# A graph attention pass on one core: the expanded target values are summed on TensorE, not on VectorE

## The reference, cut to what matters

```python
h = (x @ W).reshape(n, HEADS, HID)
src = jnp.concatenate([edge_index[0], loops])
dst = jnp.concatenate([edge_index[1], loops])
a_src = jnp.einsum('nhf,hf->nh', h, att_src)
a_dst = jnp.einsum('nhf,hf->nh', h, att_dst)
e = jax.nn.leaky_relu(a_src[src] + a_dst[dst], NEG_SLOPE)
m = jax.ops.segment_max(e, dst, num_segments=n)
ex = jnp.exp(e - m[dst])
denom = jax.ops.segment_sum(ex, dst, num_segments=n)
alpha = ex / denom[dst]
msg = h[src] * alpha[:, :, None]
agg = jax.ops.segment_sum(msg, dst, num_segments=n)
```

## Time and profile before

| | |
|---|---|
| time, 3 runs | 8511.83 us median, 8507.89 to 8514.34 |
| profiled execution, its own time | 8512.61 us |
| its span | 8510.8 us |
| busy | PE 5215.0 us, DVE 5632.1 us, ACT 3045.4 us, POOL 6107.9 us |
| granted clock of TensorE, mean | 0.755 |
| first attention pass | gathers of POOL from 2426.6 to 3591.1 us, last totals from 3654.0 us |

### The profile page before, as it was taken

The page is one execution under the profiler, slowest core; times in us unless marked ns, Lnnn a source line. Parts: engine busy times, 40 slices in busy tenths (PEclk is TensorE's granted clock), DMA queues, the critical chain, the costliest instruction groups (busy, mean ns, idle before and its releaser), DMA issues. The chain is left out here.

```text
span 8510.8 us, 132427 instructions
## 1 busy us (share of the span) xinstructions
PE 5215.0 (61%) x35514; PEld 4581.5 (54%) x35514; DVE 5632.1 (66%) x13509; ACT 3045.4 (36%) x7001; POOL 6107.9 (72%) x5620
## 2 busy tenths in 40 slices
PE   0991014444367777664444425565579898989896
PEld 0340013333345555453333325565579898989896
DVE  9661025555578888664444465555579898989898
ACT  2000002000048888632222222222156666666564
POOL 4777777777647777637777727777768787878785
PEclk7995555555578888786666657667689999999998
DMA  1671025565645555723333424444567676767674
GB/s 43 268 307 61 2 61 130 130 145 131 112 118 138 140 140 137 119 68 79 82 82 79 75 56 130 130 130 130 118 182 223 188 222 189 222 188 223 190 221 138
DMA packets 963123, 1176.14 MB, mean 138 GB/s; under 512 B 286490, under 2 KB 845422, under 8 KB 949342
## 3 DMA queue, kind: packets, MB, share of 16 engines
q1 hardware_dynamic: 806782, 864.50, 33.2%
q0 software_dynamic: 155616, 303.19, 16.8%
HBM read 897.16 MB, written 269.96 MB: 137 GB/s over the span
## 5 line engine op out<-in xcount | busy, mean ns | idle before, releaser
L2584 PE MATMUL ps<-u,wide_r 128*128 x9280 | 1141.8, 277 | 128.7 <-issue 88.6
L2584 PEld LDWEIGHTS ps<-u,wide_r 128*128 128x128 f32 x9280 | 1093.4, 194 | 130.7 <-issue 130.7
L2159 POOL DMA_INDIRECT z_r<-x_tab,src_row x880 | 851.9, 968 | 417.6 <-issue 267.8
L2596 PE MATMUL ps<-msg_r,hots_r 128*128 128x128 f32 x9280 | 1135.6, 275 | 21.6 <-POOL msg_r L2417 21.6
L2417 POOL TENSOR_TENSOR msg_r<-zo_r,share_r 128x1024 f32<-128x1024 f32 x580 | 1123.4, 1937 | 11.9 <-DVE share_r L2469 9.5
L1362 POOL DMA_INDIRECT ring_e<-t_tab,src_p x928 | 882.9, 951 | 298.8 <-issue 280.7
L2596 PEld LDWEIGHTS ps<-msg_r,hots_r 128*128 128x128 f32 x9280 | 1082.5, 192 | 26.4 <-POOL msg_r L2417 25.5
L296 POOL DMA_INDIRECT rec_tab<-pay,row_i x831 | 806.3, 970 | 372.6 <-issue 272.2
L541 POOL DMA_INDIRECT ring<-y_tab,y_row x880 | 842.8, 958 | 276.1 <-issue 263.4
L2425 POOL TENSOR_TENSOR prod_r<-prod_r 128x512 f32<-128x512 f32 x580 | 735.4, 1268 | 415.3 <-DVE prod_r L2447 414.0
L1779 POOL DMA_INDIRECT ring_e<-t_tab,src_row x880 | 830.7, 944 | 271.8 <-issue 267.8
(11 more groups left out here) (321 smaller groups left out, 9329.9 us busy)
## 6 DMA issues: line engine op xcount, KB each, us to landing
zo_r<-zo_tab SPq DMA_DIRECT2D x2320, 192.0 KB, 2.8
y_tab<-wide SPq DMA_DIRECT2D x100, 1024.0 KB, 3.9
zo_tab<-z_r SPq DMA_DIRECT2D x110, 512.0 KB
hot_bytes_e<-hb_tab SPq DMA_DIRECT2D x464, 64.0 KB
dl_b<-dl_tab SPq DMA_DIRECT2D x220, 128.0 KB, 3.7
zo_tab<-hot_bytes SPq DMA_DIRECT2D x220, 128.0 KB
hb_tab<-hot_bytes SPq DMA_DIRECT2D x220, 128.0 KB
hot_bytes_e<-hb_tab SPq DMA_DIRECT2D x55, 512.0 KB
```

The costliest lines, as they stand in the source:

```text
L2159: nc.gpsimd.indirect_dma_start(out=z[:, g % ZR, c, :], out_offset=None, in_=x3_tab, in_offset=bass.IndirectOffsetOnAxis(ap=src_row[:, g * ...
L2584: last = nc.tensor.matmul(ps[:, 2 * (g % 2) + c // 4, c % 4 * D:(c % 4 + 1) * D], wide[:, g % WR, c, :], u[:, bass.ds(tiles[g % NO % 4 * O ...
L2596: last = nc.tensor.matmul(ps[:, 4 + g % 2, c // 2 * D:(c // 2 + 1) * D], hots[:, g % WR, c, :], msg[:, g % WR, c, :], start=c % 2 == 0, st ...
```

## The change

The three parts of a value are no longer written beside one another and added by DVE. `expand` makes three matmuls of 8 columns a place, one for each part k, into the same 8 columns of PSUM: the first starts the sum (`start=k == 0`), the others add to it. The result, 16 places x 8 values, stands in columns 256 to 383 of the bank; the turned parts in columns 0 to 255 and the exponentials from column 384 stay where they were. The reduction on DVE, its semaphore `s_sent` and its SBUF tile `sent` are gone, and L1465 and L1471 read the sums from PSUM. The order in which the functions are called is the same on every engine.

```diff
-                SW = 3 * 2 * HEADS
-
-                def expanded(b):
-                    return ps[:, 6 + b % 2, 0:BC * SW]
+                def sent_of(b):
+                    return ps[:, 6 + b % 2, 256:256 + BC * 2 * HEADS].rearrange("p (c w) -> p c w", w=2 * HEADS)
...
-                            v.tensor_reduce(sent[:].rearrange("p c w -> p (c w)"),
-                                            expanded(b).rearrange("p (c k w) -> p c w k", c=BC, k=3),
-                                            AX.X, ALU.add).then_inc(s_sent, 1)
-                            dve.wait_ge(s_sent, b + 1)
-                            v.tensor_tensor(sc, sent[:, :, 0:HEADS], ring[:, b % ZR, :, hf:W], ALU.add)\
+                            v.tensor_tensor(sc, sent_of(b)[:, :, 0:HEADS], ring[:, b % ZR, :, hf:W], ALU.add)\
...
-                            v.tensor_tensor(sc, sc, sent[:, :, HEADS:2 * HEADS], ALU.subtract).then_inc(s_sc, 1)
+                            v.tensor_tensor(sc, sc, sent_of(b)[:, :, HEADS:2 * HEADS], ALU.subtract).then_inc(s_sc, 1)
...
                             for c in range(BC):
-                                last = nc.tensor.matmul(
-                                    expanded(b)[:, c * SW:(c + 1) * SW], wide[:, b % WR, c, :],
-                                    sent_b[:, b % 2, bass.ds(tiles[b][c // 2], 1)]
-                                    .rearrange("p t k w -> p (t k w)")[:, 1:2 * SW:2], start=True, stop=True)
+                                for k in range(3):
+                                    last = nc.tensor.matmul(
+                                        sent_of(b)[:, c, :], wide[:, b % WR, c, :],
+                                        sent_b[:, b % 2, bass.ds(tiles[b][c // 2], 1), k, 1:4 * HEADS:2]
+                                        .rearrange("p t w -> p (t w)"), start=k == 0, stop=k == 2)
```

More of the change, by code:

```diff
@@ L1260, in attend_running @@
                 score = sb(f"score_{name}", [P, 2, BC, HEADS], fp32, ph)
-                sent = sb(f"sent_{name}", [P, BC, 2 * HEADS], fp32, ph)
                 fade = sb(f"fade_{name}", [P, 2, HEADS], fp32, ph)
@@ L1281, in attend_running @@
                 s_exp = sem(f"expanded_{name}", ph)
-                s_sent = sem(f"expanded_parts_added_{name}", ph)
                 s_sc = sem(f"scores_{name}", ph)
```

## The result

The changed kernel takes 8538.76 us (median of 8 runs, 8531.56 to 8545.98), the kernel before 8514.30 (8 runs, 8507.89 to 8516.57). The ratio is 1.0029, interval 1.0021 to 1.0038: 24.5 us slower; 22.6 were forecast. The profiled execution of the changed kernel is the slowest of its eight, 8545.98 us (span 8544.2). Its tail will therefore show more than the median loses.

What follows compares the result with a forecast made beforehand. Gathers were taken to bound the first attention pass; the lengthened loop would outgrow them. Last gathers 17.7 us later plus three expands, 5.0 us, gave +22.6 us: 8512.6 + 22.6 = 8535 us, range 8512 to 8566.

Steps and rivals of the forecast that it cites:

- POOL's ring: First attention pass: POOL runs ahead in a ring of three batches, 10.96 us in hand, used up near batch 19.
- the stall: First pass's tail: PE stands 32.25 us for the bit lines; all loop delay beyond the last gathers' 17.7 us disappears there.
- loop's own period before: First attention pass: the loop of PE, DVE and ACT takes 18.96 us a batch, read from two recoveries.
- cover by the gathers: First attention pass: gathers take 20.10 us a batch against the loop's 18.96, so 1.14 us of lengthening is covered.
- expand, first calculation to end: PE's expand in the first pass: more address calculation steps and matmuls lengthen it by 2.24 us a batch.
- net on the loop: First attention pass: longer expand less the removed DVE reduction, 2.24 - 0.59 = +1.65 us a batch (bounds +0.16 to +2.3).
- excess a batch: First attention pass: the changed loop's 20.61 us exceeds the gathers' 20.10, so 0.51 us a batch is uncovered.
- last gathers later: End of the first pass: after its 11.0 us in hand, POOL issues the last gathers 17.7 us later.
- (1): First pass: loop still covered by the gathers, only the tail pays 0.5 to 3.4 us, 8513 to 8516; chance 0.25.
- (2): First pass: loop longer than summed, 8572; or the tail's stall doesn't swallow the ring's 11 us, +34, 8546; chance 0.10.
- (3): PE's expand: accumulating products wait for one another, +6.6 us a batch, some +300 us, 8810; chance 0.02.
- (4): First pass: faster, through shorter gathers with less work on DVE beside them, 7.4 us, 8505; chance 0.03.

Runs made afterwards that it cites:

- b_short: Kernel before with every fourth gather of the first attention pass left out from the fourth batch on: 8434.61 us, ratio 0.9913.
- e3_calcs: Kernel before plus two small matmuls a pair into unused columns, each with its own address (24 calculations, 32 matmuls a batch), DVE's sum kept: 8561.74 us, ratio 1.0058.
- e4_three: Kernel before with three products a place side by side, nothing accumulated, DVE's sum kept (24 calculations, 48 matmuls a batch): 8574.33 us, ratio 1.0076.
- a_short: Changed kernel with every fourth gather of the first attention pass left out from the fourth batch on: 8509.77 us, ratio 1.0000.
- spread runs: Kernel before and changed kernel, each with empty places gathering 128 different blank rows instead of one: 8469.95 and 8506.83 us.
- b_spread: Kernel before with empty places gathering 128 different blank rows, one a partition, instead of one and the same: 8469.95 us, ratio 0.9952.
- e2_fixed2: Changed kernel with part 2 taken from the fixed address of tile 0 (48 matmuls, 16 calculations a batch): 8510.33 us, ratio 0.9999.
- e1_fixed12: Changed kernel with parts 1 and 2 taken from the fixed address of tile 0 (48 matmuls, 8 calculations a batch): 8510.54 us, ratio 1.0001.
- a_spread: Changed kernel with empty places gathering 128 different blank rows, one a partition, instead of one and the same: 8506.83 us, ratio 0.9994.

## Why the prediction was right, and where its terms were off

The mechanism held in its steps. Expands became long through the calculations, the loop outgrew the gathers, POOL's ring was used up, the last gathers came later, and a part vanished in the stall. The sizes:

| term | forecast | measured | from |
|---|---|---|---|
| loop's own period before | 18.96 | 19.25 | b_short |
| cover by the gathers | 1.14 | 0.85 | 20.10 - 19.25 |
| expand, first calculation to end | +2.24 | +2.17 | 3.48 - 1.32, medians |
| the same, as far as the loop shows it | +2.24 | +1.99 to +2.09 | e3_calcs, e4_three less b_short |
| DVE's sum | -0.59 | -0.57 | e3_calcs less changed |
| net on the loop | +1.65 | +1.44 | a_short less b_short |
| excess a batch | 0.51 | 0.57 | changed, 20.67 - 20.10 |
| ring used up by the totals of | batch 19 | batch 16 | trace |
| POOL in hand at the last batch | 11.0 | 2.4 | before, batch 57 |
| last gathers later | 17.7 | 23.7 (25.6 from the pass's start) |, after |
| hidden by the stall | 11.0 | 12.4 by medians, 5.7 by the profiled executions | spread runs |
| whole | +22.6 | +24.5 | medians |

*Two errors in the excess nearly cancel.* The loop's own period was read 0.29 us too short. The reductions at 2607.36 and 2626.31 are single batches, and b_short shows that single batches of the free-running loop go from 18.60 to 19.89 us. The net on the loop was summed 0.2 us too long. Little of that is in the expand itself: a pair takes 0.386 us, not 0.40, and the stall of 0.1 that I added is there (0.15 us in the changed kernel, 0.06 before). From its first calculation to its end the expand grew by 2.17 us, so the rest, 0.1 to 0.2 us, is growth of the expand that the loop doesn't feel; why not, no run shows. With the first alone put right, the excess would have been 0.80 and the forecast some 15 us higher (53 x 0.29); with the second alone, 0.30 and some 11 us lower. That the forecast came within 4 us owes something to luck. The tail is a part of that: in the profiled execution, which lost 33.4 us, the last gathers came later than I had put them, and the sum fits the median of the runs better than it fits this trace.

*What would show it, point by point.* The expand shows 2.81 to 2.97 us in most batches, just below the 3.0 to 3.5 I had named; from its first calculation to its end it takes 3.42 to 3.63, since the first calculations pass before the first matmul, beside the spreads. Scores are mostly 20.56 to 20.72 us apart, as said. ACT's wait for rows falls to 16.4 us, as said. POOL waits for L1659 41.9 us, not 15 to 20. About 12 of these stood under "issue" before (277.9 us of it there, 266.3 now, the 0.30 us between two gathers). The rest, 41.9 - 1.8 - 11.6 = 28.5 us, is still more than my 17.7. (The last gathers are 25.6 us later and not 28.5, since the 928 gathers themselves took 3.3 us less, 879.6 for 882.9.) Up to batch 56 my sum is near: counted from each pass's first gather, the totals that its first gather waits for come 29.8 us later than before (28.7 in my sum), and that gather 20.5 (17.7). The step that was wrong is the last one. For batch 57 I took 11 us in hand, read at batch 31; before, POOL had 2.4 us there, in the tail's slow traffic, and so the gather comes 25.5 us later. In b_spread, without that traffic, it has 11.1 there. PE leaves the stall at 3636.9, not near 3628, for the same reason, in an execution 7 us slower than the median. The three batches after the stall cost 4.5 us more than before (3695.4 - 3636.9 for the last total's end, against 3664.4 - 3610.4), forecast 5.0.

*The rivals.* (1), still covered, failed by the 0.57 us a batch of the excess. e2_fixed2, with 16 calculations, is that case: its expand is longer than before and its time the same. In e1_fixed12 the 48 matmuls start (1.35 - 0.18) / 47 = 25 ns apart, in the changed kernel (2.95 - 0.18) / 47 = 59 ns. The first agrees with the roughly 25 ns of the Trainium skill, "TensorE: Matmul & The Clock Gate", "Wait — 56ns, not 53.3ns?"; the second shows that this floor alone doesn't price small matmuls with an address of their own. The second half of (2), that the stall swallows nothing, is wrong for the changed kernel, where a part is swallowed. In a_spread, with no stall, it is right: +36.9 us, where I had put +34. (3) is excluded by e4_three. Of (4) the half came true that gathers get shorter, a mean of 0.948 us for 0.951, 3.3 us in all, but the loop, not they, sets the pace.

*The faster version* is b_spread, 8469.95 us: 0.48% below the kernel before and some 0.8% below the changed one. It has nothing to do with the sums on TensorE. On it, too, the change loses.

## What to carry to other kernels

Before you trade an operation of one engine for small operations of another, count the address calculations, not the matmuls: a step with its own register address took 124 to 138 ns here, whether one matmul followed or four, while small matmuls without a calculation of their own started 25 ns apart. A loop hidden behind a transfer forgives an edit up to its cover and then charges the excess in each turn, so the cover has to be measured over many turns, best by taking the transfer away, rather than from one recovery. And what the tail does with a delay is a term of its own: the same change cost 24.5 us with a stall there and 36.9 without. What a buffer has in hand is to be read where it is used up, in the tail too: here it was 11 us at batch 31 and 2.4 at the last batch.

## What the hardware showed that I had not expected

- *Reads of one and the same row are slow.* Where the empty places gathered a single blank row from all partitions, a packet took 0.54 us of an engine in the mean, with 128 different rows 0.16 us, at equal sizes (6.07 MB in 2146 packets, 5.72 in 2019). The bit lines' load beside them took 33.8 us, and 15.8 with the rows spread, and the kernel ended 40 us later.
- *Accumulation is free here.* Three matmuls of 8 columns in succession into the same PSUM columns were no slower than into different ones (medians of the expand 2.92 us in both).
- *The same matmuls in another order ran at a lower granted clock:* 0.75 against 0.83, with PE busy 93% of the time instead of 84%. A higher busy share did not bring a higher clock; matmuls at the lower clock last longer, so it may in part be the clock that raised the share.
